# The turned scores ahead of the scores in each round of TensorE

## What is computed

```python
xn = _layernorm(x)
# branch 1: y = silu(scan(conv(xn @ W_in + b_in))); y @ W_out + b_out
# branch 2
q, k, v = qkv[:, :, 0], qkv[:, :, 1], qkv[:, :, 2]        # 16 heads of 16
attn = jnp.einsum('bqhd,bkhd->bhqk', q, k) / sqrt(16)
attn_out = jnp.einsum('bhqk,bkhd->bqhd', softmax(attn), v)
# branch 3
gate = softmax(x @ W_gate + b_gate)                        # the two largest of 8
moe_out = einsum('bsef,bse->bsf', x @ W_experts + b_experts, combine)
return x + branch1 + attn_out + moe_out
```

## Time and profile before

| | before |
|---|---|
| median of three runs | 788.93 us (787.6 to 789.32) |
| the profiled execution | 787.89 us |
| its span, first to last instruction | 786.1 us |
| TensorE matmul busy | 753.9 us, 96% |
| VectorE busy | 581.4 us, 74% |
| ScalarE busy | 535.4 us, 68% |
| GpSimd busy | 387.4 us, 49% |
| maxima (L1051) | 256, mean 1222 ns |
| exponentials (L830) | 251 from TB, mean 1027 ns |

### The profile page before, as it was taken

The page is one execution under the profiler, slowest core; times in us unless marked ns, Lnnn a source line. Parts: engine busy times, 40 slices in busy tenths (PEclk is TensorE's granted clock), DMA queues, the critical chain, the costliest instruction groups (busy, mean ns, idle before and its releaser), DMA issues.

```text
span 786.1 us, 13228 instructions
## 1 busy us (share of the span) xinstructions
PE 753.9 (96%) x4404; PEld 453.3 (58%) x4404; DVE 581.4 (74%) x846; ACT 535.4 (68%) x926; POOL 387.4 (49%) x522
## 2 busy tenths in 40 slices
PE   9689999999998999999999999989999999999996
PEld 7457556565555655556555665556655565555553
DVE  6689876976679875887759876698667987568920
ACT  4637766777666767667567775667666776767775
POOL 8445554455444834456346463445444473435654
PEclk9989999999999999999999999999999999999999
DMA  8301201122110221102111121113111121112000
GB/s 272 69 4 44 68 19 28 38 59 78 35 38 13 79 58 41 42 22 82 35 42 42 45 82 31 38 25 95 42 42 43 32 58 39 46 41 69 23 2 27
DMA packets 32465, 39.09 MB, mean 50 GB/s; under 512 B 8513, under 2 KB 18535, under 8 KB 32398
## 3 DMA queue, kind: packets, MB, share of 16 engines
q1 hardware_dynamic: 31418, 37.29, 18.1%
q10 hardware_dynamic: 980, 0.96, 0.6%
HBM read 8.74 MB, written 4.19 MB: 16 GB/s over the span
## 4 chain that ended last, share of the span: by engine, by line
PE 80%; DVE 13%; issue 4%; ACT 3%; ACTq 0%; DVEq 0%
PE PS L464 39%; PE PS L624 12%; PE SB L591 12%; PE TB L608 7%; PE PS L521 5%; DVE mx L1051 4%; PE PS L480 2%; DVE ys L901 2%; DVE xn L1027 1%; PE PS L631 1%; DVE xl L933 1%; DVE qkl L927 1%; DVE ys L897 1%; PE PS L476 1%; DVE th L1086 1%
## 5 line engine op out<-in xcount | busy, mean ns | idle before, releaser
L1051 DVE TENSOR_REDUCE mx<-SB 128x2 f32<-128x1024 f32 x256 | 312.9, 1222 | 141.0 <-PE SB L591 139.9
L1118 POOL TENSOR_TENSOR acc<-acc,mt 128x256 f32<-128x256 f32 x320 | 247.9, 782 | 251.0 <-ACT mt L675 178.9
L830 ACT ACTIVATE Pt<-TB 128x1024 f32<-128x1024 f32 x251 | 257.7, 1027 | 59.3 <-PE TB L608 56.3
L675 ACT ACTIVATE mt<-PS,cpad 128x256 f32<-128x256 f32 x256 | 107.5, 471 | 58.9 <-PE PS L464 58.5
L591 PE MATMUL SB<-kst,qst 48*128 48x512 f32 x512 | 127.9, 496 | 14.6 <-DVE mx L1051 14.3
L624 PE MATMUL PS<-Pt,V 128*17 128x512 f32 x1024 | 122.3, 595 | 0.0
L591 PEld LDWEIGHTS SB<-kst,qst 48*128 48x128 f32 x512 | 47.7, 183 | 125.3 <-DVE mx L1051 75.1
L464 PE MATMUL PS<-weh,xTh 128*128 128x512 f32 x256 | 109.9, 429 | 2.2 <-DVE xTl L914 1.3
L608 PE MATMUL TB<-qst,kst 50*128 50x512 f32 x502 | 101.2, 398 | 1.1 <-ACT Pt L830 1.0
L464 PE MATMUL PS<-wel,xTh 128*128 128x512 f32 x256 | 100.9, 394 | 0.0
L464 PE MATMUL PS<-weh,xTl 128*128 128x512 f32 x256 | 100.6, 393 | 0.0
(11 more groups left out here) (162 smaller groups left out, 1142.6 us busy)
## 6 DMA issues: line engine op xcount, KB each, us to landing
qst<-qkh SPq DMA_DIRECT2D x124, 64.0 KB, 2.3
kst<-qkh SPq DMA_DIRECT2D x124, 64.0 KB, 2.3
out<-acc SPq DMA_DIRECT2D x8, 512.0 KB, 2.8
qst<-qkl SPq DMA_DIRECT2D x62, 64.0 KB, 2.2
kst<-qkl SPq DMA_DIRECT2D x62, 64.0 KB, 2.3
acc<-in_x SPq DMA_DIRECT2D x7, 512.0 KB, 3.9
Bt<-in_wexp SPq DMA_DIRECT2D x2, 512.0 KB, 7.6
raw<-in_wexp SPq DMA_DIRECT2D x2, 512.0 KB, 8.8
```

The source lines that it names most:

```text
L675: return e.activation(mt[:, item % NM, :], P, ACT.Copy, scale=scale)
L830: e.activation(Pt[:, T % NP, :, :], turned_bank(T)[:, :, :], ACT.Exp, scale=0.25).then_inc(s_ex, 1)
L1051: e.tensor_reduce(mx[:, g % 2, 0:2, 4 * jj + a], SB[:, :, :], AX.X, ALU.max).then_inc(s_mx, 1)
L1118: e.tensor_tensor(v, v, mt[:, item % NM, :], ALU.add).then_inc(s_mt, 1)
```

## The change

In the loop over rounds, the call of `turned` and its condition move ahead of the call of `score`. The same instructions are issued with the same waits. In rounds 11 to 255 both calls are there, and the two matmuls of the turned product come before the two of the score; in the other rounds only one of them is there, or none.

```diff
             for t in range(-1, END):
+                if LAG <= t < STEPS + LAG:
+                    turned(t - LAG)
                 if 0 <= t < STEPS:
                     score(t)
-                if LAG <= t < STEPS + LAG:
-                    turned(t - LAG)
                 for m in values_at(t):
                     values(m)
```

## The result

The kernel after takes 791.98 us (median of five runs, 790.85 to 792.73), the kernel before in the same session 788.93. The ratio is 1.0039, with a 95% interval of 1.0028 to 1.0051. The profiled execution has a span of 789.1 us, where before it was 786.1.

The account below looks back on a forecast made before the run. TensorE, busy 96% of the span, was taken as the bound, so only its standing times could move. Terms of -1.05, +1.9, +0.35 and +0.85 summed to +2.05 us over 788.93: 791.0 us, own range 789.5 to 793, 8-in-10 range 787.9 to 794.0.

Parts of the forecast that it names:

- The price of a place: On TensorE, a pair takes 0.66 us from first load to next work; each place is worth 0.23 us of streaming.
- e+0.66, M+0.43: Pair's end after the change: 0.66 us past its earliest first load (e), 0.43 past the maxima's arrival (M), whichever is later.
- Late maxima: Where score loads wait for row maxima made late by something else, 0.23 us gained each: sum -1.05 us.
- The nine on a score loop: Nine of 25 late maxima ending a VectorE backlog begun at a score: the maxima move 0.23 later too, gain 0.
- the second rival: Turned product fills the score load's wait for maxima, all 25 gaining 0.23 us: 784, or 786.5 with half; chance 0.10.
- Late exponentials: Where the turned load waits for a late exponential, put first it loses up to 0.47 us: sum +1.9 us.
- another 0.23: At late exponentials, the convolution's last tap stands behind a VectorE maximum starting 0.23 us later, adding 0.23 to the loss.
- SP's rows: SP writes maxima into the stack, last at 577.61 us; the turned load put first loses 0.23 to 0.47, taken as +0.35.
- VectorE's units: Units behind a later maximum on VectorE: three or four lose 0.23 us, one 0.14; +0.85 us, bounds 0 and 1.8.
- The last rival: VectorE's later start runs taps into GpSimd's additions, a fifth more taps losing 0.4 us: 795 us; chance 0.13.
- the taps' mean: Sign: convolution taps' mean of 0.92 us should stay within 0.02; growth of 0.05 or more would show VectorE-GpSimd contention.
- The first rival: Everything turns together: rotating two neighbours in a round changes no binding distance; 788.9 us, give or take 1.2; chance 0.27.

Follow-up runs that it names:

- GpSimd short: Additions into `acc` cut to 32 of 256 columns, low parts of x and y likewise from the second batch: 781.01 us in the order of before, 782.17 of after.
- the kernel with the late exponentials: Turned product first in only six rounds (24, 68, 76, 79, 208, 212) of the kernel before: 789.79 us, ratio 1.0011.

## Why the prediction was right, and where by luck

The kernel after took 791.98 us where 791.0 was forecast, and the change costs time, as forecast. The terms fared differently.

**The price of a place** holds. In the kernel after, at round 119 (timeline, beside the earlier trace rows):

```profile
384.45 1.22 DVE L1051 TENSOR_REDUCE mx<-SB 128x2 f32<-128x1024 f32 x1
384.60 0.19 PEld L608 LDWEIGHTS TB<-qst,kst 50*128 50x128 f32 x2 [0.36 <-issue]
385.72 0.19 PEld L591 LDWEIGHTS SB<-kst,qst 48*128 48x128 f32 x2 [0.94 <-DVE mx L1051]
386.15 0.13 PEld L624 LDWEIGHTS PS<-Pt,V 128*17 128x17 f32 x8 [0.24 <-issue]
```

The maximum isn't earlier against its round, the turned product has gone into the wait, and 0.24 us is saved behind it. That is e+0.66, M+0.43, as written. The four stretches forecast with the whole 0.23 gave 0.21 to 0.26.

**Late maxima** were over-valued all the same, -0.5 for -1.05. Three stretches with a second limit in them (154, 340 and 433 us) gave it back and 0.11 to 0.17 more. The nine on a score loop gave nothing beyond some 0.1 us, as forecast, and this is what the second rival denied; it would have needed -3 us or more. That 23 of the rounds gain 1.5 to 2.5 us when only they are swapped is another matter: there the scores of the other rounds, and with them VectorE's queue, aren't later.

**Late exponentials.** 684 us gave +0.12 for 0.14, and 184 and 737, forecast at 0.05 and 0.10, nothing that can be told from 0. At 107 the term was more than twice too large: +0.19 for 0.47. The rows there, in the kernel after, beside the earlier trace rows:

```profile
104.98 0.63 ACT L753 ACTIVATE th<-ys 128x512 f32<-128x512 f32 x1 [1.62 <-DVE ys L901]
...
106.39 1.01 ACT L830 ACTIVATE Pt<-TB 128x1024 f32<-128x1024 f32 x1
...
107.46 0.19 PEld L608 LDWEIGHTS TB<-qst,kst 50*128 50x128 f32 x2 [1.73 <-ACT Pt L830]
108.12 0.11 PEld L476 LDWEIGHTS PS<-ident,mx 128*72 128x72 f32 x1 [0.36 <-issue]
```

From the turned load to the next work it is 0.66 us instead of 0.44, and the place's price is all there. VectorE's share isn't: the tanh is 0.33 us later by the clock, which is what the whole program had lost by then, so it hasn't moved against its round. What kept it is the tap one round earlier. Before, and then after:

```profile
100.20 1.85 DVE L901 SCALAR_TENSOR_TENSOR ys<-uc,cwc,ys 128x510 f32<-128x510 f32 x1
100.21 1.30 POOL L1239 TENSOR_TENSOR yl<-th,yh 128x512 fp32r<-128x512 f32 x1
```

```profile
100.55 1.29 POOL L1239 TENSOR_TENSOR yl<-th,yh 128x512 fp32r<-128x512 f32 x1
...
100.78 1.61 DVE L901 SCALAR_TENSOR_TENSOR ys<-uc,cwc,ys 128x510 f32<-128x510 f32 x1
```

The maximum ahead of this tap did follow its score, and the tap begins 0.24 us later against its round. But it ends 0.55 us behind the end of the same GpSimd instruction in both kernels, so it takes 1.61 instead of 1.85 and hands nothing on. This is the step of the prediction that was mis-sized: "another 0.23" asks that VectorE's shift travel down its queue to the tanh, and a tap that already waited for GpSimd swallows it. With GpSimd short, the same tap begins 0.23 later against its round, takes 0.86 in either order, and the round costs 0.41. From round 11 on, 96 taps (L897 and L901) begin 0.15 us or more later against their round, and 34 of them end at most 0.05 later; before the change, every one of the 34 ended 0.54 to 0.55 us behind a GpSimd instruction.

At 636 us, forecast 0.35, it was 0.09, for the same reason. The last two taps ahead of the tanh begin 0.24 and 0.22 later against their rounds and end where they did, behind the same two GpSimd instructions. They took 0.99 and 1.04 us before and take 0.75 and 0.80 in the timeline of after:

```profile
630.98 0.75 DVE L901 SCALAR_TENSOR_TENSOR ys<-uc,cwc,ys 128x510 f32<-128x510 f32 x1
...
633.64 0.80 DVE L901 SCALAR_TENSOR_TENSOR ys<-uc,cwc,ys 128x509 f32<-128x509 f32 x1
634.47 0.63 ACT L753 ACTIVATE th<-ys 128x512 f32<-128x512 f32 x1 [0.68 <-DVE ys L901]
```

At 648, 714 and 744 it went the other way, by 0.4, 0.3 and 1.0.

**SP's rows** cost nothing for 0.35. Before, one of SP's issues ahead of the earlier trace rows took 1.49 us (at 575.42); after, the same one took 0.67, the last row was issued at 577.05, and the turned load at 579.51 didn't wait. I had taken the place of a DMA issue as fixed. Of the 14 traces, only before and the one with GpSimd short and the order of before (1.38 us) have a long issue there; twelve have 0.67, five of them with the order of before at this place. So the order alone doesn't make it, and the term was read from an execution that had the rarer case. Whether the term would be there otherwise isn't shown.

**VectorE's units** were right at 69.9 and 253.8 us (0.24 and 0.27 for 0.23), and nothing at 618 and 639. There too a tap had swallowed the shift. The one at 600.29 us begins 0.24 later against its round and takes 0.89 us instead of 1.14, and from it to the earlier trace rows's `ml` all of VectorE's rows are back at their place; for 639 it is the tap at 635.50, 0.78 instead of 1.05.

**The last rival** is the mechanism of more than half the loss, and in its reverse, the swallowed shift, of what the forecast lost elsewhere. The forecast gave it 795 us, from a fifth more of the taps being longer. What came is a mean *shorter* by 0.04 us, 0.88 instead of 0.92, and three taps longer at the places that count: 10 taps are over 0.1 us longer than before, 46 over 0.1 shorter, since one that begins later behind the same GpSimd instruction ends at the same time. The point from which it decides was put rightly in the prediction (longer taps on rounds whose tanh is already tight), and the sign to look for was put wrongly: the taps' mean. It should have been the taps ahead of tight tanhs, one by one. That the time fell into the range is partly luck. The total of 2.05 us came out near 3 because swallowed shifts took away about 0.9 us of the forecast (107, 636, 618 and 639: 0.28, 0.26, 0.23 and 0.14) and the absent wait for SP's rows 0.35, while collisions newly met added 1.6 to 1.8 and the late maxima gained 0.5 less.

The Trainium skill (GPSIMD Engine Reference, Specifications) names the sharing of SBUF interfaces and the contention at VectorE instructions with two SBUF inputs. The traces agree in kind: taps that meet nothing of GpSimd take at most 0.75 us, those that do up to 1.75 after the change and 1.85 before, and the maxima, which read PSUM, take 1.19 to 1.23 either way.

**The first rival** (788.9, everything turns together) is excluded by both sessions, 1.0028 and 1.0019 at the lowest, but much of its picture is true: against its round's first load the maxima start 0.24 later in the median and the tanh only 0.085, with single ones from 0.37 earlier to 0.96 later. The forecast sign "0.2 later" for the tanh was wrong, for the reason just given: the end of a tap that runs into GpSimd is set by GpSimd and not by its own start.

**Still open** is some 1 us of the timings. The same kernel was 3.05 and 1.97 us slower in two sessions with overlapping intervals, and the steps can't tell more than that the order of instructions gives 2.85 to 3.0. Whether the rounds near 154, 340 and 433 us lose by a unit of VectorE or by the exponential was not taken apart.

## What to carry to other kernels

Swapping two neighbours in the bottleneck's order pays in the rounds where the one is late and costs in the rounds where the other is, so swap those rounds and leave the rest: 23 rounds chosen from the waits gave 0.997 where all 245 gave 1.0039. When a change shifts an engine by a few tenths of a microsecond, look at what it shares with others: a collision can swallow the shift as well as enlarge it. Follow single instructions ahead of the tight waits, since a mean can fall while the three that count grow. To see where a small difference is made, subtract the starts of one repeated instruction between the two traces, round by round; busy times and sums of waits could not show it here.

## What the runs showed of the hardware

A tap of the convolution on VectorE (three operands, two of them tiles of 128x509 to 128x511 in SBUF) takes 0.73 to 0.75 us alone. If it begins while an addition or subtraction of GpSimd into `acc`, `xl` or `yl` is under way, it ends 0.54 to 0.55 us behind that instruction's end, whenever it began: 1.20 us at 645.15 behind an addition, 1.75 at 740.92 behind a 1.28 us subtraction that began 0.08 earlier. With under 0.2 us of GpSimd's instruction left, it takes its 0.73 to 0.75 all the same. It doesn't seem slowed but held up.

A tap that begins first is let through if its lead is large enough, and then it is GpSimd that waits: 0.74 us at 739.07 in the kernel before, where the subtraction that began 0.36 later took 1.52 instead of 1.28. A lead of a few hundredths isn't enough. In the kernel before, nine taps begin 0.01 to 0.03 us ahead, and eight of them take 1.30 to 1.32 us and one 1.85; the smallest lead that was let through is 0.14 there and 0.07 in the kernel after. So the loss depends on a few hundredths of a microsecond in the starts. With GpSimd short the kernel is 8 us faster, 1%.

The granted clock of executions of the same order isn't the same. All of them have half the clock (1.2 instead of 2.4 GHz) for 6.8 us between 35 and 46 us. Four of the 14 traces have it once more for about 3 us near 50 us, as after has here (window, columns as in the earlier trace rows):

```profile
50.00:53.00 3.00, 3.00 (x8) 1.64 (x7) 2.93 (x6) 0.85 (x2) 2.73 (x3) 0.51 0.00 0
```

where the kernel before has 1.00. This costs 0.35 to 0.55 us before round 11, at a place where the programs don't differ. With what the start of the program varies by itself, the executions stand between 0.35 us ahead of before and 1.41 behind it at round 11, and that is why steps are counted from there. The other case, at 521.8 us among the late exponentials, came behind a standing time of 1.65 us of TensorE, which the kernel before has too, at 519.33, without losing the clock. It cost 1.0 us, a third of the effect that was to be measured. Neither dip can be seen in the page's row of clocks: those of after and of the kernel with the late exponentials are digit for digit the one in the earlier trace rows.
